# A four-layer transformer on one core: in the first layer the shared key and value heads are projected once and spread afterwards

## What is computed

```python
D, H, HKV = 256, 16, 4
HD, REP = D // H, H // HKV                      # 16 columns a head, 4 query heads to one key head
q = (h @ wq.T).reshape(b, n, HKV, REP, HD)      # wq: 256 x 256
k = (h @ wk.T).reshape(b, n, HKV, HD)           # wk: 64 x 256
v = (h @ wv.T).reshape(b, n, HKV, HD)           # wv: 64 x 256
scores = jnp.einsum('bqgrh,bkgh->bgrqk', q, k) * (1.0 / np.sqrt(HD))
a = jax.nn.softmax(scores, axis=-1)
out = jnp.einsum('bgrqk,bkgh->bqgrh', a, v).reshape(b, n, d)
```

## Time and profile before

| | |
|---|---|
| median of 3 runs | 2399.96 us (2397.11 to 2403.16) |
| the profiled execution, its own time | 2402.53 us |
| its span, first to last instruction | 2400.7 us |
| TensorE matmuls busy | 2240.4 us, 93% |
| VectorE, ScalarE, GpSimd busy | 69%, 52%, 45% |
| mean granted TensorE clock | 0.989 of 2.4 GHz |

### The profile page before, as it was taken

How to read it: one execution, slowest core, us unless ns; L and a number is a source line. 1 busy time by engine, 2 the same in 40 slices (tenths; PEclk the granted TensorE clock), 3 DMA queues, 4 the chain that set the end, 5 groups by cost and what they waited for, 6 DMA issues and landing times.

```text
span 2400.7 us, 63280 instructions
## 1 busy us (share of the span) xinstructions
PE 2240.4 (93%) x20392; PEld 1859.2 (77%) x20392; DVE 1660.3 (69%) x3866; ACT 1254.3 (52%) x2620; POOL 1089.8 (45%) x1333
## 2 busy tenths in 40 slices
PE   7699999999999999999999999999999999999997
PEld 5477887778777877877877777777778787888877
DVE  3567666677666556556677666766788888888873
ACT  0366556656554554555566555656564434444442
POOL 1244454445444444444554444444554454444433
PEclk9899999999999999999999999999999999999998
DMA  6221112212221121122232112112222212121210
GB/s 210 92 70 61 59 62 68 68 59 74 84 84 54 58 68 50 58 68 64 77 107 70 56 60 70 61 56 69 72 89 64 66 54 70 53 70 51 72 54 14
DMA packets 164960, 166.12 MB, mean 69 GB/s; under 512 B 29329, under 2 KB 144401, under 8 KB 164849
## 3 DMA queue, kind: packets, MB, share of 16 engines
q1 hardware_dynamic: 164848, 164.69, 21.5%
HBM read 58.47 MB, written 4.39 MB: 26 GB/s over the span
## 4 chain that ended last, share of the span: by engine, by line
PE 58%; issue 14%; POOL 10%; DVE 9%; ACT 4%; SPq 1%; POOLq 1%; DMA 0%; DVEq 0%; ACTq 0%
PE B L482 25%; PE B L587 8%; PE B L741 6%; PE B L530 5%; PE B L716 5%; POOL GHl L1244 5%; PE B L507 3%; PE B L596 3%; ACT PR L890 3%; DVE NEGM L961 3%; PE B L606 1%; POOL H1l L1289 1%; POOL X L1230 1%; PE B L689 1%; DVE HF L1087 1%
## 5 line engine op out<-in xcount | busy, mean ns | idle before, releaser
L890 ACT ACTIVATE PR<-B 128x512 f32<-128x512 f32 (+1 forms) x1024 | 506.7, 564 | 339.1 <-PE B L716 230.6
L1244 POOL TENSOR_TENSOR GHl<-G,GHh 128x256 fp32r<-128x256 f32 x512 | 378.0, 739 | 481.8 <-ACT GHh L863 327.6
L961 DVE TENSOR_REDUCE NEGM<-B 128x2 f32<-128x512 f32 x768 | 477.7, 683 | 61.2 <-PE B L530 60.4
L482 PE MATMUL B<-H2h,W1h 128*128 128x256 f32 x1280 | 394.8, 308 | 3.2 <-issue 3.1
L863 ACT ACTIVATE G<-B,VEC 128x256 f32<-128x256 f32 x384 | 182.1, 474 | 359.5 <-PE B L482 356.9
L482 PE MATMUL B<-H2h,W1l 128*128 128x256 f32 x1280 | 362.9, 283 | 0.0
L482 PE MATMUL B<-H2l,W1h 128*128 128x256 f32 x1280 | 362.4, 283 | 0.0
L587 PE MATMUL B<-W2h,GHh 128*128 128x256 f32 x1024 | 299.3, 292 | 3.5 <-POOL GHl L1244 3.5
L741 PE MATMUL B<-PR,V 128*32 128x256 f32 (+1 forms) x4096 | 261.3, 373 | 36.3 <-ACT PR L890 29.4
L587 PE MATMUL B<-W2l,GHh 128*128 128x256 f32 x1024 | 289.5, 283 | 0.0
L587 PE MATMUL B<-W2h,GHl 128*128 128x256 f32 x1024 | 288.8, 282 | 0.0
(11 more groups left out here) (148 smaller groups left out, 4813.2 us busy)
## 6 DMA issues: line engine op xcount, KB each, us to landing
QS<-QHL SPq DMA_DIRECT2D x768, 64.0 KB, 2.1
KS<-KHL SPq DMA_DIRECT2D x768, 64.0 KB, 2.1
GA<-gate_scratch SPq DMA_DIRECT2D x48, 256.0 KB, 3.2
GM<-gate_scratch SPq DMA_DIRECT2D x48, 256.0 KB, 3.3
RAW<-in_w SPq DMA_DIRECT2D x36, 256.0 KB, 3.2
CW<-in_cw SPq DMA_DIRECT2D x3, 1536.0 KB, 13.7
X<-in_x SPq DMA_DIRECT2D x2, 2048.0 KB, 10.2
QS<-MT SPq DMA_DIRECT2D x256, 4.0 KB
```

Of the source, the lines that this page charges most:

```text
L482: last = nc.tensor.matmul(dst, w[i], x[j], start=(first_k and n == 0), stop=(last_k and n == 2))
L890: nc.scalar.activation(PR[:, h % PRING].rearrange("p k q -> p (k q)")[:, 0:n], src[:, 0:n], ACT.Exp, scale=SCALE).then_inc(ac_exp, 1)
L961: last = nc.vector.tensor_reduce(NEGM[:, :, c], src, op=ALU.max, axis=AX.X, negate=True)
L1244: nc.gpsimd.tensor_tensor(GH[1][:, j % RING, :], G[:, j % RING, :], GH[0][:, j % RING, :].bitcast(F32), ALU.subtract).then_inc(po_gl, 1)
```

## The change

For layer 0 the key and value weights keep their own 64 columns each. Key: one column block of 64 in place of two of 128, so 6 matmuls in place of 12, and `KHL` is filled in 64 partitions and one block. The DMAs that stack `KS` read each of the 32 partitions of a group twice, by a dimension with stride 0; their number and the 64 KB that each moves stay. Value: 12 matmuls as before, with 64 moving columns in place of 256; VectorE's copy to `VT` has 64 columns for each of the two token blocks, and GpSimd's move is two instructions, one a token block, each spreading 4 heads to 16 places. The first weights are two chunks in place of four.

```diff
+HKV = 4
+DKV = HKV * HD
+WQ_COLS = (D + 2 * DKV, 3 * D, 3 * D, 3 * D)
...
-        first_weights = part(0, "q", 0, 1, 2, 3) + part(0, "o", 0)
+        first_weights = part(0, "q", 0, 1) + part(0, "o", 0)
...
-                    if s.q is None:
+                    if s.q is None or (s.lq == 0 and f > 0):
                         return
...
-                    last = project(bank(3)[:, f, :], cols(wq, D + f * P), H1)
-                    if f == KD - 1:
+                    if s.lq == 0:
+                        last = project(bank(3)[0:DKV, 0, :], [v[:, :, D:D + DKV] for v in wq], H1)
+                    else:
+                        last = project(bank(3)[:, f, :], cols(wq, D + f * P), H1)
+                    if s.lq == 0 or f == KD - 1:
                         last.then_inc(pe_k, 1)
...
-                        last = product(bank(2)[:, i, :], [x[:, k, i * P:(i + 1) * P] for x in H1],
-                                       [w[:, k, 2 * D:3 * D] for w in wq], k == 0, k == KD - 1)
+                        v = slice(D + DKV, D + 2 * DKV) if s.lq == 0 else slice(2 * D, 3 * D)
+                        last = product(bank(2)[:, i, 0:v.stop - v.start], [x[:, k, i * P:(i + 1) * P] for x in H1],
+                                       [w[:, k, v] for w in wq], k == 0, k == KD - 1)
...
-                    nc.vector.tensor_copy(VT[:], bank(2)).then_inc(dv_v, 1)
+                    width = DKV if s.lq == 0 else D
+                    nc.vector.tensor_copy(VT[:, :, 0:width], bank(2)[:, :, 0:width]).then_inc(dv_v, 1)
...
+                    few = s.lq == 0 and dst is KHL
+                    src, hi, lo = (v[0:DKV, 0, :] if few else v for v in (bank(nbank), dst[:, 0], dst[:, 1]))
+                    nc.vector.tensor_copy(hi, src).then_inc(s_hi, 1)
                     dv.wait_ge(s_hi, s.q + 1)
...
-                    nc.gpsimd.tensor_copy(V_HEADS[:, :, :, 0:HD], VT[:].rearrange("p i (h d) -> p i h d", h=H)).then_inc(po_v, 1)
+                    if s.lq == 0:
+                        for i in range(NT):
+                            shared = V_HEADS[:, i, :, 0:HD].rearrange("p (g r) d -> p g r d", g=HKV)
+                            heads = VT[:, i, 0:DKV].rearrange("p (g d) -> p g d", g=HKV).unsqueeze(2)
+                            last = nc.gpsimd.tensor_copy(shared, heads.to_broadcast([P, HKV, H // HKV, HD]))
...
-                                sp.dma_start(dst[rows_r, slots, :].bitcast(F32),
-                                             src[ROWS * group:ROWS * group + ROWS, x, half, :].bitcast(F32)).then_inc(
-                                                 sp_stk[group], 16)
+                                if s.lq == 0 and dst is KS:
+                                    shared = src[DKV // 2 * group:DKV // 2 * (group + 1), x, 0:1, :]
+                                    heads = shared.to_broadcast([DKV // 2, HKV // 2, T])
+                                else:
+                                    heads = src[ROWS * group:ROWS * group + ROWS, x, half, :]
+                                sp.dma_start(dst[rows_r, slots, :].bitcast(F32), heads.bitcast(F32)).then_inc(sp_stk[group], 16)
```

More of the change, by code:

```diff
@@ L54 @@
 QKV_BIAS = (False, False, True, True)
-WQ_COLS = (3 * D,) * NL
+HKV = 4
+DKV = HKV * HD
+WQ_COLS = (D + 2 * DKV, 3 * D, 3 * D, 3 * D)
 W1_COLS = (DFF, DFF, DFF, 2 * DFF)
@@ L1190, in split_qk @@
                 else:
-                    nc.vector.tensor_copy(dst[:, 0], bank(nbank)).then_inc(s_hi, 1)
+                    few = s.lq == 0 and dst is KHL
+                    src, hi, lo = (v[0:DKV, 0, :] if few else v for v in (bank(nbank), dst[:, 0], dst[:, 1]))
+                    nc.vector.tensor_copy(hi, src).then_inc(s_hi, 1)
                     dv.wait_ge(s_hi, s.q + 1)
-                    nc.vector.tensor_tensor(dst[:, 1], bank(nbank), dst[:, 0].bitcast(F32), ALU.subtract).then_inc(s_lo, 1)
+                    nc.vector.tensor_tensor(lo, src, hi.bitcast(F32), ALU.subtract).then_inc(s_lo, 1)
             steps(dv, body)
@@ L1282, in body @@
                     apart(po)
-                    nc.gpsimd.tensor_copy(V_HEADS[:, :, :, 0:HD], VT[:].rearrange("p i (h d) -> p i h d", h=H)).then_inc(po_v, 1)
+                    if s.lq == 0:
[4 more added lines that the diff above has]
+                    else:
+                        last = nc.gpsimd.tensor_copy(V_HEADS[:, :, :, 0:HD], VT[:].rearrange("p i (h d) -> p i h d", h=H))
+                    last.then_inc(po_v, 1)
             def low_1(s):
@@ L1372, in lay_out @@
     d["cw_t1"], d["cw_t2"] = g["L3_cond_w_t1"], g["L3_cond_w_t2"]
-    rep = H // 4
-    def spread(w):
-        return np.repeat(w.T.reshape(D, 4, 1, HD), rep, axis=2).reshape(D, D)
     f, g_, d_, h_ = np.meshgrid(np.arange(KD), np.arange(2), np.arange(HD), np.arange(HG), indexing="ij")
@@ L1384, in stacked @@
         return np.concatenate([q[:, paired], k[:, paired], v], axis=1)
-    d["wq0"] = stacked(g["L0_cond_wq"].T, spread(g["L0_cond_wk"]), spread(g["L0_cond_wv"]))
+    g_, d_, h_ = np.meshgrid(np.arange(2), np.arange(HD), np.arange(HKV // 2), indexing="ij")
+    shared = ((HKV // 2 * g_ + h_) * HD + d_).reshape(-1)
+    d["wq0"] = np.concatenate([g["L0_cond_wq"].T[:, paired], g["L0_cond_wk"].T[:, shared], g["L0_cond_wv"].T], axis=1)
     d["wq1"], d["wq2"] = (stacked(*np.split(g[f"L{l}_cond_Wqkv"], 3, axis=1)) for l in (1, 2))
```

## The result

| | before | changed |
|---|---|---|
| median of 4 runs | 2398.93 us (2397.11 to 2403.16) | 2429.97 us (2427.06 to 2432.55) |
| the profiled execution, its own time | 2402.53 us | 2427.86 us |
| its span | 2400.7 us | 2425.0 us |
| mean granted TensorE clock | 0.989 | 0.964 |

The kernel before was run once more beside the changed one, so its median here is of four runs. The ratio is 1.0126, with a 95% interval of 1.0106 to 1.0147. The forecast was 2398.0, the range 2390 to 2404: it was wrong by 32 us, and no rival had this sign for the reason that holds.

What follows compares the result with a forecast made beforehand. It took layer 0's steps to be bound by what ends the waits behind keys and values, chiefly VectorE's maxima. Keys -1.0 and values -1.0, all else 0, gave -2.0 us: 2398.0 us, range 2390 to 2404.

Steps and rivals of the forecast that it cites:

- What bounds the kernel: Layer 0's steps: TensorE 95% busy at clock 1.00, but what ends the wait behind keys and values decides the gain.
- chain of maxima: VectorE's last four maxima beside the key matmuls, ending 0.13 us before the transposes, so saved key time is mostly hidden.
- cover: Other work hiding savings or costs: TensorE's own list hides VectorE's shorter splits; GpSimd's moves have slack before `GHl`.
- B: Value matmuls in layer 0's tail cost by their moving columns: 8.5 us saved, 2391.5 us, chance 0.09.
- C: TensorE is the bound outright, all its saved work in layer 0 is gained: 12.8 us, 2387 us, chance 0.06.
- D: GpSimd's two moves of V outlast the 1.6 us allowed and delay the next step: 21 us, 2421 us, chance 0.05.
- Start-up: Program start: two weight chunks fewer cost 0; clock from 56 to 96 us bounded at 1 to 2 us slower, taken as 0.
- Keys: Six fewer key matmuls in layer 0: gain 0 to 0.13 us a step, taken as 0.07, 1.0 us in all.
- Values: Second six value matmuls, between pairs 2 and 3, at 0.109 us apart: 0.07 us a step, 1.0 us in all.
- VectorE, GpSimd, stacks: Shorter splits and copy, two moves of V, and the K stacks' DMAs: each taken as 0 on the time.

Runs made afterwards that it cites:

- e5: The kernel before, untouched, run once more for a second profile: 2401.48 us for 2396.33, ratio 1.0014.
- e2: The changed kernel with value matmuls streaming 256 columns again, only the last 64 used, keys still 6 matmuls: 2402.06 us, ratio 1.0019 to the kernel before.
- e4: The changed kernel with the 6 key matmuls issued twice and value matmuls of 256 columns: 2395.99 us, ratio 0.9994 to the kernel before.
- e3: The changed kernel with the 6 key matmuls issued twice, value matmuls still 64 columns: 2408.41 us, ratio 1.0057 to the kernel before.
- e11: The changed kernel with layer 0's second query block moved behind the last score pairs, both value blocks narrow: 2406.56 us, ratio 1.0035 to the kernel before.
- e8: The changed kernel with the first value block wide, keys once, layer 0's second query block behind the last score pairs: 2386.75 us, ratio 0.9960 to before.

## Why the prediction was wrong

- **What bounds the kernel**: right for steps at a clock of 1.00. Waits, chain of maxima and cover behave as the earlier trace rows said. The rivals B, C and D all fell: values did not cost by their columns, saved keys were not gained, and the moves of V took 0.74 us of the 1.6 allowed.
- **The step that failed** is the one on the clock, in "Start-up". It bounded what fewer matmuls do to the clock at "1 to 2 us slower", and only for the stretch from 56 to 96 us. In the loop it put the clock at nothing without giving a reason: it took the 1.00 of the earlier trace rows as a property of the place, when it is the answer to the work put there. The runs put 27 to 30 us on that in layer 0 (527.0 and 529.0 us in the two profiles of the change, 499.0 and 500.3 in those of the kernel before). The rows of before held a hint: from 56 to 96 us TensorE was busy 19 of 40 us and its clock 0.79 (0.68 in `e5`, where the record reaches back further), which suggests that the clock answers to how TensorE is occupied in this very kernel. The forecast read it, and did not ask it of the part that it was making thinner. A rival E was missing: fewer and narrower matmuls lower the clock; if it fell once in each of the 15 steps and cost 1.5 to 4 us each time, as the steps now show, 22 to 60 us. The forecast could have sized one such fall by half speed over some microseconds of the tail.
- **Keys**: forecast 0.07 us a step, measured 0 (33.44 and 33.45 in `e2` and `e4`). The transposes follow the last maximum by 0.13 us in either case; that is the price of the release, and nothing of it was to be had.
- **Values**: forecast 0.07, measured 0.11 to 0.13 (33.43 a step before, 33.30 to 33.32 on average at a clock of 1.00 with the second block narrow). The distance came out at 0.112 us, near the 0.109 of the forecast, and that is the smaller part. From the start of the second block to pair 3 it is 330.45 - 329.55 = 0.90 us before and 297.02 - 296.24 = 0.78 with the change, and 0.09 of the 0.12 lies in one place: the second matmul of the block starts 0.22 us behind the first before (329.55, 329.78) and 0.13 behind it with the change. The earlier trace rows was misread in this: the 0.219 us for 16 columns belongs to the 1.2 GHz level, and it is no agreement with the 107 ns that the prediction sets beside it. The same 32 matmuls in `e5`'s trace, and others of the same shape from 38 us on, where the recorded clock is 0.50:

```profile
12.71 3.98 PE L358 MATMUL B<-SC,CW 128*128 128x16 f32 x32
...
38.35 7.01 PE L358 MATMUL B<-Z,X 128*128 128x16 f32 x32 [1.01 <-DVE Z L379]
```

  In the first row the clock rises after the first few; from the fourth on they start 0.112 us apart, as the value matmuls with 64 columns do. Matmuls with 16 and with 64 moving columns at the same distance mean that the columns do not set it. So the choice of 0.109 stood, on a wrong ground.
- **VectorE, GpSimd, stacks**: 0 on the time, as forecast, shown by `e2` and `e4` against the kernel before. The stacks' DMAs are not free for all that: for the same bytes the busy share of the DMA engines in the ten steps is 0.20 before and 0.23 in `e2` and `e4`. An issue still takes 0.60 us and lands in 2.1, and nothing waits for them.

The Trainium skill has a rule for the clock that would have come out as the forecast did: in "TensorE: Matmul & The Clock Gate", "Why this matters for your kernels", it warns of long idle gaps of TensorE between matmuls. The changed kernel has none: its longest wait in the ten steps is 1.0 us, and yet the clock fell nine times from 155 to 514 us. The same page's section "A second HAM failure mode: psum-queue depth-cycling" tells of a kernel whose TensorE idles often and briefly and whose clock oscillates for it. The oscillating clock is what this case shows, with a mean of 0.90 and waits of 0.2 to 1.0 us; that short waits alone bring it this case does not bear out, as `e2` shows below.

```profile
PE B L747 <- ACT PR L896: 6.4, 10, 1.0
PE B L722 <- ACT PR L896: 3.9, 9, 0.4
PE B L722 <- DVE NEGM L967: 2.5, 9, 0.3
PE B L484 <- POOL H1l L1305: 2.2, 9, 0.2
PE B L695 <- DVE NEGM L967: 1.5, 9, 0.2
```

These are the changed kernel's waits of TensorE from 194 to 528.3 us (total us, times, longest). Waits alone are not enough: `e2` has the same ones, 8.6, 3.0, 2.9, 2.5 and 1.7 us, at a clock of 1.00. Nor are the new waits behind the keys needed for a fall. `e3` has none before pairs 0 and 1 and fell seven times; its waits in the tail, apart from the 8.9 us before the outputs, are

```profile
PE B L723 <- ACT PR L897: 4.0, 9, 0.4
PE B L696 <- DVE NEGM L968: 1.5, 9, 0.2
```

What all runs with falls in the loop share is value matmuls of 64 or 128 columns in the first block, with nothing added behind it, and a wait of 0.4 us before pair 2. Whether narrow matmuls without that wait would bring a fall no run shows.

## What to carry to other kernels

In this kernel a granted clock of 1.00 in a stretch turned out to be a result of the work that stands there. When a change makes TensorE's work thinner, put "the clock falls" among the cases, price it with durations of the same instructions at the 1.2 GHz level, and look at the clock column of the changed stretch first. If it fell, give the engine back some work inside a wait that it has anyway, and reorder so that the freed time is used (the reordering alone, `e11`, did not end the falls, and with one wide value block, `e8`, it made the kernel faster); before either, ask which chain ends beside the removed work, since that decides whether there is any time to be had.

## What the runs showed that was not expected

- With four unread matmuls of 192 columns a step the program took 34 us less: 2431.85 us and 2397.80, measured on two chips on which the kernel before took 2396.03 and 2396.33. TensorE with more to do was sooner done.
- With 64 moving columns and a weight load each, matmuls start 0.112 us apart at the 2.4 GHz level and 0.21 at the 1.2 GHz level; 16 columns 0.112 and 0.219; 256 columns 0.12 us at the 2.4 GHz level. Narrowing from 256 to 64 buys 7%.
- Two moves of 256 columns on GpSimd take 0.74 us together, one of 512 took 0.61; a DMA that reads a partition's row twice by a stride of 0 took no longer to issue and to land than one that reads two rows, but kept the DMA engines busier, 0.23 for 0.20 over all transfers (`e2`, `e4`).
- The falls came in every step of `e11` (each step 34.1 us) and in some steps of the change (33.3 to 37.3 us), for the same work in another order. Within a step they begin at nearly the same place in both, 1.8 to 3.4 us behind the second maxima transposes.
